# Reordering the opening of a one-core cross-attention and FFN kernel: other matmuls between a tile and its reader, waits at the readers, Wo group 0 beside Wq

## The chip, the cores and the metric

The kernel runs on one core of a Trainium2 chip, and its time is the device time of one execution in microseconds. Three executions of the kernel before took 855.80, 855.86 and 856.62 us (median 855.86).

## What is computed

Eight batches of 128 tokens of width 512 are normalised, attend with 32 query heads (4 key/value heads, head size 128) over a context of 128 rows per batch and over themselves, and go through a gated FFN with fake-quantised weights and activations. Cut to what matters:

```
hidden = concat([context, latents], axis=1)            # latents = layernorm(x)
q = (latents @ Wq)   # 512 x 4096: 4 groups of 8 heads
k, v = hidden @ Wk, hidden @ Wv                         # 512 x 512 each
attn = softmax(einsum('bqhgd,bkhd->bhgqk', q, k) / sqrt(128))
x = x + (attn @ v).reshape(b, q_len, 4096) @ Wo
x = x + ffn(layernorm(x))   # gate, up, down with block-quantised weights, act_qdq between
```

## The kernel before, in words

Every f32 operand is split into an upper f16 part, written by ScalarE (`hi`, L552), and a lower f16 part, written by VectorE (`lo`, L742), and every product is three f16 matmuls (`three`, L313). All reads of a PSUM bank by these two together are called its eviction here; the buffer is free once VectorE's half is through.

All order is written out by hand, engine by engine; waits are counts on semaphores. Each engine's program of the opening walks the same 32 slots, one per key or value tile:

- slots 0 to 7: keys of the context (the first four interleaved by contraction chunk, L351 to L359), slots 8 to 15: its values, with the transposes of the normalised x between them from slot 12 on (`transpose_x`);
- slots 16 to 23: keys of x (`k_tile`), in banks 0 to 3. ScalarE and VectorE evict the tile and split one piece of Wq group 0 (`wq_upper`, `wq_lower`) in each slot;
- then query tiles 0 to 3 (`q_first`, `q_second`, two heads each, banks 6 and 7), scores 0 and 1 (`scores`, banks 0 to 3), on the other engines all ahead of slot 24;
- slots 24 to 31: values of x, eight tiles of 12 matmuls in banks 4 and 5 (the loop `for i in range(B)` of the tensor program). One piece of Wo group 0 is split in each slot (`wo_upper`, `wo_lower`). Reciprocals, products with them (`normalise`, GpSimd) and the splits of P for steps 0 and 1, and the stages of weight unit 3, lie between (`units_in`; a unit is a 128 x 512 piece of an FFN weight that is quantised here and stored to DRAM);
- query tiles 4 and 5, and the loop over 64 steps.

A loop step t holds scores t+2, the Wo product of step t-1 (`project`), query tile t+6 and the product with the values (`head_out`), whose operand comes through a DMA transpose of P (`turn_p`, issued by SP). SP also issues every load, in program order. Wq and Wo pieces have two landing buffers each, so a load n of either waits until piece n-2 is split. `keep_warm` multiplies zeros into a bank that nobody reads.

Its counters in the waits that the change touches: `kv_free` rises by one with each evicted key or value tile and starts at 4 (28: all keys of x are out, 35 and 36: value tiles 6 and 7 too); `q_lo` rises with each evicted query tile; scores 0 want 2, scores 1 want 4; query tile f wants f-1, its bank's last user.

Of the kernel before, what the change touches and what calls it, by code (L numbers as in the profile page):

```python
# [19 lines left out]
B, T, H = 8, 128, 512  # L20
# [61 lines left out]
def build(nc, x, ctx_t, wq, wk, wv, wo, w_units, w_ready, out):  # L82
    stack = ExitStack()
    with stack:
# [94 lines left out]
        kv_mm, kv_hi, kv_free = sem("kv_mm"), sem("kv_hi"), sem("kv_free")  # L179
# [44 lines left out]
        def _(sp):  # L224
# [12 lines left out]
            def load_wo(n):  # L237
                if n >= 2:
                    sp.wait_ge(wo_lo, n - 1)
                sp.dma_start(wo_raw[:, n % 2], wo[n * D:(n + 1) * D, :]).then_inc(wo_loaded[n % 2], 16)  # L240
# [23 lines left out]
            for slot in range(32):  # L264
                if 17 < slot <= 23:
                    load_wq(slot - 16)
                if 25 < slot <= 31:
                    load_wo(slot - 24)
                for v in units_in(slot, 4):
                    store_unit(v)  # L270
                for v in units_in(slot, 1):
                    load_unit(v + 1)
# [39 lines left out]
        def _(pe):  # L312
# [29 lines left out]
            def keep_warm(n):  # L342

                for _ in range(n):
                    nc.tensor.matmul(banks[OB][:, :], warm[:, 0:P], warm[:, :], start=True, stop=True)  # L345

            pe.wait_ge(warm_set, 1)
            keep_warm(8)

            pe.wait_ge(kv_free, NG)  # L350
            for c in range(HC):  # L351
# [31 lines left out]
            def q_first(f):  # L383

                if f % QUADS < 4:
                    pe.wait_ge(wq_lo, f // QUADS * GH + 2 * (f % QUADS) + 2)
                if f >= 2:
                    pe.wait_ge(q_lo, f - 1)
                q_head(f, 0)

            def q_second(f):

                q_head(f, 1).then_inc(q_mm, 1)
# [18 lines left out]
            def head_out(t):  # L412

                g, b = t // QUADS, t % QUADS // 2
                pe.wait_ge(pt_loaded[t % 2], 16 * (t // 2 + 1))
                for c in range(2):
                    for n, (i, r) in enumerate(((0, 0), (0, 1), (1, 0))):
                        mm = nc.tensor.matmul(banks[OB][:, :], kv[:, g + 1, 2 + i, (c * B + b) * P:(c * B + b + 1) * P],  # L418
                                              pt_s[:, t % 2, r, c, :], start=c == 0 and n == 0, stop=c == 1 and n == 2)
                mm.then_inc(pv_mm, 1)  # L420

            def project(t):

                par, hq = t // QUADS % 2, t % 2
                if t % QUADS == 0:
                    pe.wait_ge(wo_lo, t // QUADS * GH + GH)
                if hq == 0 and t >= 2:
                    pe.wait_ge(y_add, t // 2)
                pe.wait_ge(o_hi, t + 1)
                for hh in range(4):  # L430
                    for r in range(2):
                        nc.tensor.matmul(banks[YB][:, :], o_s[:, 0, hh * P:(hh + 1) * P], wo_s[:, par, r, hq * 4 + hh, :],  # L432
                                         start=hq == 0 and hh == 0 and r == 0, stop=False)
                pe.wait_ge(o_lo, t + 1)
                for hh in range(4):
                    mm = nc.tensor.matmul(banks[YB][:, :], o_s[:, 1, hh * P:(hh + 1) * P], wo_s[:, par, 0, hq * 4 + hh, :],  # L436
                                          start=False, stop=hq == 1 and hh == 3)
                mm.then_inc(wo_mm, 1)
# [6 lines left out]
                    mm = nc.tensor.transpose(banks[QB + b % 2][:, c * P:(c + 1) * P], xln2[:, b, c * P:(c + 1) * P], ident[:, :])  # L445
                mm.then_inc(x2_mm, 1)

            pe.wait_ge(xt_free, 12)
            pe.wait_ge(kv_free, 28)
            for f in range(4):  # L450
                q_first(f)
                q_second(f)
                if f == 1:
                    scores(0)
                if f == 3:
                    scores(1)
            for i in range(B):
                if i >= 2:
                    pe.wait_ge(kv_free, 27 + i)
                three(banks[OB + i % 2][:, :], lambda r, c: src_t[:, 5, r, c, i * P:(i + 1) * P],  # L460
                      lambda r, c: wkv_s[:, 1, r, c, :], HC).then_inc(kv_mm, 1)
            for f in range(4, Q_AHEAD):
                q_first(f)
                q_second(f)
            pe.wait_ge(kv_free, 36)
            for t in range(STEPS):
                f = t + Q_AHEAD
                if t + AHEAD < STEPS:
# [81 lines left out]
        def _(act):  # L550
# [67 lines left out]
            for slot in range(32):  # L618
                if slot == 24:
                    q_upper(0)  # L620
                    q_upper(1)
                    exps(0)
                    q_upper(2)
                    q_upper(3)
                    exps(1)
                if slot < 8:
                    k_hi(slot + 1, 0, slot // 4, slot % 4, slot)
                elif slot < 16:
                    v_hi(slot + 1, (slot - 8) * P, slot % 4)
                    if slot >= 12:  # L630
                        xt_upper(2 * (slot - 12))
                        xt_upper(2 * (slot - 12) + 1)
                elif slot < 24:
                    if slot == 16:
                        act.wait_ge(wv_lo, 1)
                    k_hi(slot + 1, 1, (slot - 16) // 4, slot % 4, slot % 4)
                    wq_upper(slot - 16)
                else:
                    v_hi(slot + 1, TOK + (slot - 24) * P, OB + slot % 2)
                    wo_upper(slot - 24)  # L640
                for v in units_in(slot, 2):
                    unit_hi(v)
                if slot == 25:
                    p_upper(0)
# [94 lines left out]
        def _(dve):  # L739
# [136 lines left out]
            for slot in range(32):  # L876
# [10 lines left out]
                if slot == 24:  # L887
                    q_lower(0)
                    q_lower(1)
                    maxima(0)  # L890
                    q_lower(2)
                    reciprocals(0)
                    q_lower(3)
                    maxima(1)
                if slot < 8:
                    k_lo(slot + 1, 0, slot // 4, slot % 4, slot)
                    if slot == 0:
                        dve.wait_ge(x_loaded, 16)
                    nc.vector.bn_stats(bn[:, slot, :], y[:, slot, :]).then_inc(ln_stat, 1)
                elif slot < 16:  # L900
                    v_lo(slot + 1, (slot - 8) * P, slot % 4)
                    if slot >= 12:
                        xt_lower(2 * (slot - 12))
                        xt_lower(2 * (slot - 12) + 1)
                elif slot < 24:
                    k_lo(slot + 1, 1, (slot - 16) // 4, slot % 4, slot % 4)
                    wq_lower(slot - 16)
                else:
                    v_lo(slot + 1, TOK + (slot - 24) * P, OB + slot % 2)
                    wo_lower(slot - 24)  # L910
                if slot == 25:
                    reciprocals(1)
                if slot == 26:
# [331 lines left out]
```

## Time and profile before

| | us |
|---|---|
| median of three executions | 855.86 |
| the profiled execution: span | 855.7 |
| lowest and highest of the three | 855.80, 856.62 |
| opening up to the loop's first matmul | 119.96 |
| attention loop to the last step's products | about 120 to 619 |
| FFN | about 628 to the end |
| PE busy | 786.4 |
| VectorE, ScalarE, GpSimd busy | 630.4, 456.0, 248.8 |

The profiled execution has no time of its own beside its span, which lies 0.16 us under the median. The page gives busy time by engine and by fortieths of the span. A timeline gives instructions in order of time, neighbours of one line merged, with the idle time of their engine ahead of them in brackets. A view by stage gives busy time in chosen stretches, with the granted TensorE clock.

### The profile page before, as it was taken

What the parts mean: (1) busy time and instruction counts of PE and PEld (TensorE: products, weight loads), DVE (VectorE), ACT (ScalarE), POOL (GpSimd) and SP (SyncE); (2) the same over time, 40 slices, a digit from 0 to 9 for tenths busy, and PEclk for the clock granted to TensorE, in tenths of its full rate; (3) what the DMA queues carried; (4) which work ended last, traced back from release to release, by engine and by line L of the source; (5) the groups of instructions that cost most, each with busy time, mean ns of one, the idle gap of its engine ahead of it and who ended that gap; (6) DMA issues with size and microseconds to landing.
All of it is one profiled execution on the core that took longest, in us unless ns stands there. A gap on an engine that the chain in (4) does not pass through costs nothing. (4 is left out here: it accounts for less than half of the span.)

```text
span 855.7 us, 12659 instructions
## 1 busy us (share of the span) xinstructions
PE 786.4 (92%) x4747; PEld 467.2 (55%) x4747; DVE 630.4 (74%) x1148; ACT 456.0 (53%) x968; POOL 248.8 (29%) x380
## 2 busy tenths in 40 slices
PE   8998999999999999999999999998799999701998
PEld 3455466666666666666666666664344444300443
DVE  5874467888777778767878778997485589999741
ACT  5253456655656555656655555554340079695730
POOL 0210313356334455443366334343100012112000
PEclk9999999999999999999999999999899999955999
DMA  9121155757446665465575458787270000000010
GB/s 317 64 75 50 42 131 119 170 133 160 99 111 148 160 139 142 91 150 134 140 169 124 95 128 162 143 171 142 51 135 0 1 1 1 0 1 0 25 38 37
DMA packets 203437, 85.50 MB, mean 100 GB/s; under 512 B 170352, under 2 KB 186736, under 8 KB 203376
## 3 DMA queue, kind: packets, MB, share of 16 engines
q1 hardware_dynamic: 203376, 84.69, 43.3%
q8 instruction: 37, 0.61, 0.3%
q14 instruction: 24, 0.20, 0.1%
HBM read 31.72 MB, written 10.75 MB: 50 GB/s over the span
## 5 line engine op out<-in xcount | busy, mean ns | idle before, releaser
L318 PE MATMUL bank<-arena 128*128 128x256 f16 (+1 forms) x1872 | 261.0, 292 | 3.7 <-DVE arena L742 2.1
L318 PEld LDWEIGHTS bank<-arena 128*128 128x128 f16 x1872 | 182.8, 98 | 85.5 <-DVE arena L742 3.7
L1127 POOL TENSOR_SCALAR arena<-arena,rsum 128x256 f32<-128x256 f32 x256 | 132.7, 518 | 312.0 <-DVE rsum L808 297.9
L742 DVE SCALAR_TENSOR_TENSOR arena<-bank,arena 128x512 f16<-128x512 f32 x168 | 114.7, 689 | 117.7 <-ACT arena L552 117.3
L552 ACT ACTIVATE arena<-bank 128x512 f16<-128x512 f32 x168 | 98.8, 598 | 172.6 <-PE bank L418 95.6
L742 DVE SCALAR_TENSOR_TENSOR arena<-arena 128x512 f16<-128x512 f32 (+4 forms) x196 | 171.4, 886 | 15.8 <-ACT arena L552 15.6
L552 ACT ACTIVATE arena<-arena 128x512 f16<-128x512 f32 (+5 forms) x172 | 135.5, 809 | 61.2 <-POOL arena L1127 19.1
L594 ACT ACTIVATE arena<-bank,nmax 128x256 f32<-128x256 f32 x256 | 117.6, 471 | 60.3 <-DVE nmax L800 60.1
L432 PE MATMUL bank<-arena 128*128 128x512 f16 x512 | 122.7, 383 | 1.5 <-ACT arena L552 1.5
L494 PE MATMUL bank<-arena 128*128 128x512 f16 x528 | 114.1, 379 | 0.0
L408 PE MATMUL bank<-arena 128*128 128x256 f16 x768 | 94.3, 273 | 2.8 <-DVE arena L742 2.8
L418 PE MATMUL bank<-arena 128*128 128x512 f16 x384 | 93.4, 379 | 2.8 <-DMA arena<-arena 2.8
L494 PEld LDWEIGHTS bank<-arena 128*128 128x128 f16 x528 | 51.7, 98 | 62.3 <-issue 0.2
L408 PEld LDWEIGHTS bank<-arena 128*128 128x128 f16 x768 | 75.0, 98 | 12.7 <-DVE arena L742 3.4
L797 DVE TENSOR_REDUCE nraw<-bank 128x4 f32<-128x1024 f32 x64 | 78.3, 1224 | 3.2 <-PE bank L408 3.2
L432 PEld LDWEIGHTS bank<-arena 128*128 128x128 f16 x512 | 50.2, 99 | 50.4 <-issue 2.5
L436 PE MATMUL bank<-arena 128*128 128x512 f16 x256 | 66.2, 381 | 0.0
L669 ACT ACTIVATE arena<-arena,qc 128x1024 int32<-128x1024 f32 (+5 forms) x58 | 55.5, 986 | 16.4 <-DVE qc L990 16.4
L345 PE MATMUL bank<-warm 128*128 128x512 f16 x48 | 17.2, 534 | 47.9 <-DVE worst L968 46.5
L418 PEld LDWEIGHTS bank<-arena 128*128 128x128 f16 x384 | 37.2, 98 | 36.7 <-DMA arena<-arena 4.7
L544 PE MATMUL bank<-arena 128*128 128x512 f16 x264 | 57.1, 379 | 0.0
L594 ACT ACTIVATION_READ_ACCUMULATOR arena<-bank,nmax 128x1 f32 x256 | 51.8, 203 | 0.0
(99 smaller groups left out, 579.6 us busy)
## 6 DMA issues: line engine op xcount, KB each, us to landing
arena<-in_w_units SPq DMA_DIRECT2D x33, 256.0 KB, 3.6
w_ready<-arena SPq DMA_DIRECT2D x33, 256.0 KB, 3.2
arena<-in_wq SPq DMA_DIRECT2D x32, 256.0 KB, 3.5
arena<-in_wo SPq DMA_DIRECT2D x32, 256.0 KB, 3.6
arena<-in_x SPq DMA_DIRECT2D x1, 2048.0 KB, 15.0
out<-arena SPq DMA_DIRECT2D x8, 256.0 KB, 2.0
arena<-in_wk SPq DMA_DIRECT2D x4, 256.0 KB, 4.8
arena<-in_ctx_t SPq DMA_DIRECT2D x4, 256.0 KB, 5.4
```

The source lines that it names most:

```text
L318: last = nc.tensor.matmul(bank, a(i, c), b(j, c), start=start and c == 0 and n == 0, stop=stop and c == chunks - 1 and n == 2)
L408: mm = nc.tensor.matmul(o, q_s[:, buf, i, h, (b % 2) * P:(b % 2) * P + P], kv5[:, g + 1, r, :, b * P:(b + 1) * P], start=n == 0, stop=n == 2)
L418: mm = nc.tensor.matmul(banks[OB][:, :], kv[:, g + 1, 2 + i, (c * B + b) * P:(c * B + b + 1) * P], pt_s[:, t % 2, r, c, :], start=c == 0 a ...
L432: nc.tensor.matmul(banks[YB][:, :], o_s[:, 0, hh * P:(hh + 1) * P], wo_s[:, par, r, hq * 4 + hh, :], start=hq == 0 and hh == 0 and r == 0, ...
L436: mm = nc.tensor.matmul(banks[YB][:, :], o_s[:, 1, hh * P:(hh + 1) * P], wo_s[:, par, 0, hq * 4 + hh, :], start=False, stop=hq == 1 and hh ...
L494: mm = nc.tensor.matmul(banks[t % 4][:, :], wgu[:, m * FT + t, i, c * P:(c + 1) * P], xq[:, j, c, th * 512:(th + 1) * 512], start=c == 0 a ...
L544: mm = nc.tensor.matmul(banks[b % 4][:, :], oq[:, h, t, b * P:(b + 1) * P], wd_s[:, t, r, :], start=t == 0 and m == 0, stop=t == FT - 1 an ...
L552: return nc.scalar.activation(dst, src, ACT.Copy, scale=scale)
L594: nc.scalar.activation(p_s[:, t % 2, :, hh, :], bank[:, (hh % 2) * 256:(hh % 2) * 256 + 256].rearrange("p (c t) -> p c t", c=2), ACT.Exp, ...
L742: return nc.vector.scalar_tensor_tensor(out=dst, in0=src, scalar=scale, in1=part, op0=ALU.mult, op1=ALU.subtract)
L797: nc.vector.tensor_reduce(nraw[:, :], psum[:, s:s + 2, :].rearrange("p b (h t) -> p (b h) t", h=2), AX.X, ALU.max, negate=True).then_inc(n ...
L1127: done = nc.gpsimd.tensor_scalar(p_s[:, t % 2, :, hh, :], p_s[:, t % 2, :, hh, :], rsum[:, t % 2, hh:hh + 1], P_SCALE, ALU.mult, ALU.mult)
```

## The change

- TensorE: query tiles 0 to 2, then the wait for all keys of x, scores 0, query tile 3, value tile 0 of x, scores 1, value tiles 1 to 7. The wait for all value evictions ahead of the loop becomes two, in `head_out` and `project` of step 0.
- ScalarE and VectorE follow that order: exponentials and maxima of step 0 behind the eviction of query tile 2, those of step 1 behind the eviction of value tile 0.
- Wo group 0 is loaded and split in slots 16 to 23 beside Wq.
- Ten matmuls on zeros at the start instead of eight.

```
@@ sync
             for slot in range(32):
                 if 17 < slot <= 23:
                     load_wq(slot - 16)
-                if 25 < slot <= 31:
-                    load_wo(slot - 24)
+                    load_wo(slot - 16)
@@ tensor
-            keep_warm(8)
+            keep_warm(10)
@@ head_out
+                if t == 0:
+                    pe.wait_ge(kv_free, 35)
@@ project
+                if t == 0:
+                    pe.wait_ge(kv_free, 36)
@@ tensor
-            pe.wait_ge(xt_free, 12)
-            pe.wait_ge(kv_free, 28)
-            for f in range(4):
-                q_first(f)
-                q_second(f)
-                if f == 1:
-                    scores(0)
-                if f == 3:
-                    scores(1)
-            for i in range(B):
+            def x_value_tile(i):
+
                 if i >= 2:
                     pe.wait_ge(kv_free, 27 + i)
                 three(banks[OB + i % 2][:, :], lambda r, c: src_t[:, 5, r, c, i * P:(i + 1) * P],
                       lambda r, c: wkv_s[:, 1, r, c, :], HC).then_inc(kv_mm, 1)
+
+            pe.wait_ge(xt_free, 12)
+            for f in range(3):
+                q_first(f)
+                q_second(f)
+            pe.wait_ge(kv_free, 28)
+            scores(0)
+            q_first(3)
+            q_second(3)
+            x_value_tile(0)
+            scores(1)
+            for i in range(1, B):
+                x_value_tile(i)
             for f in range(4, Q_AHEAD):
                 q_first(f)
                 q_second(f)
-            pe.wait_ge(kv_free, 36)
@@ scalar, slot 24
                     q_upper(0)
                     q_upper(1)
+                    q_upper(2)
                     exps(0)
-                    q_upper(2)
                     q_upper(3)
-                    exps(1)
@@ scalar, slots 16 to 23, then 24 to 31
                     wq_upper(slot - 16)
+                    wo_upper(slot - 16)
                 else:
                     v_hi(slot + 1, TOK + (slot - 24) * P, OB + slot % 2)
-                    wo_upper(slot - 24)
+                    if slot == 24:
+                        exps(1)
@@ vector, slot 24
                     q_lower(0)
                     q_lower(1)
+                    q_lower(2)
                     maxima(0)
-                    q_lower(2)
                     reciprocals(0)
                     q_lower(3)
-                    maxima(1)
@@ vector, slots 16 to 23, then 24 to 31
                     wq_lower(slot - 16)
+                    wo_lower(slot - 16)
                 else:
                     v_lo(slot + 1, TOK + (slot - 24) * P, OB + slot % 2)
-                    wo_lower(slot - 24)
+                    if slot == 24:
+                        maxima(1)
```

TensorE from the last keys of x to the loop, before. The 128x256 rows of L318 are query tiles (24 matmuls each), its 128x512 rows are key and value tiles (12 each), L408 is a score step:

```order
L318 MATMUL bank<-arena 128x512 x96
L318 MATMUL bank<-arena 128x256 x48
L408 MATMUL bank<-arena 128x256 x12
L318 MATMUL bank<-arena 128x256 x48
L408 MATMUL bank<-arena 128x256 x12
L318 MATMUL bank<-arena 128x512 x96
L318 MATMUL bank<-arena 128x256 x48
L408 MATMUL bank<-arena 128x256 x12
```

The same stretch in the changed kernel, where these lines are L317 and L407:

```order
L317 MATMUL bank<-arena 128x512 x96
L317 MATMUL bank<-arena 128x256 x72
L407 MATMUL bank<-arena 128x256 x12
L317 MATMUL bank<-arena 128x256 x24
L317 MATMUL bank<-arena 128x512 x12
L407 MATMUL bank<-arena 128x256 x12
L317 MATMUL bank<-arena 128x512 x84
L317 MATMUL bank<-arena 128x256 x48
L407 MATMUL bank<-arena 128x256 x12
```

A third query tile now stands ahead of scores 0, and a value tile between query tile 3 and scores 1. No matmul is added or lost here.

SP from the first in-slot load of Wq (L235) to the first transpose of P (L254), before; L245 and L249 are the load and the store of a weight unit:

```order
L235 DMA arena<-in_wq 128x4x128 x6
L240 DMA arena<-in_wo 128x512
L245 DMA arena<-in_w_units 128x512
L240 DMA arena<-in_wo 128x512 x3
L249 DMA w_ready<-arena 128x1024
L240 DMA arena<-in_wo 128x512 x2
L254 DMA_TRANSPOSE arena<-arena 128x16x128
```

And changed:

```order
L235 DMA arena<-in_wq 128x4x128
L240 DMA arena<-in_wo 128x512
L235 DMA arena<-in_wq 128x4x128
L240 DMA arena<-in_wo 128x512
L235 DMA arena<-in_wq 128x4x128
L240 DMA arena<-in_wo 128x512
L235 DMA arena<-in_wq 128x4x128
L240 DMA arena<-in_wo 128x512
L235 DMA arena<-in_wq 128x4x128
L240 DMA arena<-in_wo 128x512
L235 DMA arena<-in_wq 128x4x128
L240 DMA arena<-in_wo 128x512
```

Here the loads of Wo alternate with those of Wq; behind them come a unit's load, its store and the first transpose, with nothing between.

ScalarE from query tile 0 on, before (L552 is `hi`, of a bank 128x512 a query tile, of a bank 128x4x128 a value tile, of the arena 128x512 a Wo piece, 128x1024 P; L594 the exponentials):

```order
L552 ACTIVATE arena<-bank 128x512 x2
L594 ACTIVATE arena,psums<-bank,nmax 128x2x128 x4
L552 ACTIVATE arena<-bank 128x512 x2
L594 ACTIVATE arena,psums<-bank,nmax 128x2x128 x4
L552 ACTIVATE arena<-bank 128x4x128
L552 ACTIVATE arena<-arena 128x512
L552 ACTIVATE arena<-bank 128x4x128
L552 ACTIVATE arena<-arena 128x512
L552 ACTIVATE arena<-arena 128x1024
```

And changed, where the lines are L559 and L601:

```order
L559 ACTIVATE arena<-bank 128x512 x3
L601 ACTIVATE arena,psums<-bank,nmax 128x2x128 x4
L559 ACTIVATE arena<-bank 128x512
L559 ACTIVATE arena<-bank 128x4x128
L601 ACTIVATE arena,psums<-bank,nmax 128x2x128 x4
L559 ACTIVATE arena<-bank 128x4x128
L559 ACTIVATE arena<-arena 128x1024
L559 ACTIVATE arena<-bank 128x4x128 x2
```

No Wo piece stands between the value tiles any more, the exponentials of step 0 stand ahead of the eviction of query tile 3, and those of step 1 ahead of the eviction of value tile 1.

## Rows read from the trace of the kernel before

**Rows 1.** The page: busy us, share of the span, instructions of TensorE.
```profile
PE 786.4 (92%) x4747; PEld 467.2 (55%) x4747; DVE 630.4 (74%) x1148; ACT 456.0 (53%) x968; POOL 248.8 (29%) x380
```
**Rows 2.** By stage: window, length, busy us of each engine, granted clock, DMA share, GB/s.
```profile
9.90:18.00 8.10, 8.10 (x39) 3.70 (x38) 4.42 (x5) 5.20 (x6) 0.50 (x1) 1.00 1.05 392
120.00:520.00 400.00, 400.00 (x2770) 270.76 (x2768) 311.16 (x540) 237.97 (x612) 179.89 (x280) 1.00 0.59 133
603.00:607.00 4.00, 4.00 (x10) 1.36 (x9) 1.23 (x1) 1.90 (x3) 0.00 (x0) 0.50 0.21 42
```
**Rows 3.** Timeline of TensorE: start, us, what, count, [idle before it <- releaser].
```profile
52.92 20.88 PE L318 MATMUL bank<-arena 128*128 128x512 f16 x96
75.26 5.40 PE L318 MATMUL bank<-arena 128*128 128x256 f16 x48 [1.46 <-issue]
82.08 1.48 PE L408 MATMUL bank<-arena 128*128 128x256 f16 x12 [1.42 <-DVE arena L742]
...
90.21 1.48 PE L408 MATMUL bank<-arena 128*128 128x256 f16 x12 [1.42 <-DVE arena L742]
91.53 13.11 PE L318 MATMUL bank<-arena 128*128 128x512 f16 x60
105.24 2.76 PE L318 MATMUL bank<-arena 128*128 128x512 f16 x12 [0.59 <-DVE arena L742]
109.53 10.59 PE L318 MATMUL bank<-arena 128*128 128x512 f16 x72 [1.53 <-DVE arena L742]
119.96 1.47 PE L408 MATMUL bank<-arena 128*128 128x256 f16 x12
```
**Rows 4.** Timeline of ScalarE, then of VectorE, between 74 and 108 us.
```profile
85.06 0.47 ACT L594 ACTIVATE arena<-bank,nmax 128x256 f32<-128x256 f32 x1 [3.77 <-DVE nmax L800]
...
86.87 0.61 ACT L552 ACTIVATE arena<-bank 128x512 f16<-128x512 f32 x1
...
107.12 1.15 ACT L552 ACTIVATE arena<-arena 128x512 f16<-128x512 f32 x2 [4.43 <-DMA arena<-in_wo]
...
74.47 0.69 DVE L742 SCALAR_TENSOR_TENSOR arena<-bank,arena 128x512 f16<-128x512 f32 x1 [1.30 <-ACT arena L552]
...
100.74 2.02 DVE L742 SCALAR_TENSOR_TENSOR arena<-arena 128x512 f16<-128x512 f32 x2
```
**Rows 5.** GpSimd: timeline at 99 us, then all 33 of L1151 (ns min/median/max).
```profile
99.01 2.67 POOL L1127 TENSOR_SCALAR arena<-arena,rsum 128x256 f32<-128x256 f32 x4 [8.49 <-DVE rsum L808]
101.76 1.90 POOL L1151 TENSOR_TENSOR arena<-arena,winv 128x512 f32<-128x512 f32 x1
...
L1151 POOL TENSOR_TENSOR arena<-arena,winv x33: 1046/1048/1897, 28.9 to 565.4; 128x512 f32<-128x512 f32 x33
```
**Rows 6.** SP's issues of Wo at 104 us; landings of L240, 90 to 600, then all.
```profile
104.07 4.76 SPq L240 DMA_DIRECT2D arena<-in_wo  x3
...
DMA to landing us min/median/max: 2.5/3.6/5.1
...
DMA to landing us min/median/max: 2.5/3.6/10.6
```
**Rows 7.** Timeline of the first 40 us: TensorE, its weight loads, VectorE.
```profile
1.44 3.59 PE L345 MATMUL bank<-warm 128*128 128x512 f16 x8 [1.44 <-POOL warm L1118]
5.77 12.47 PE L356 MATMUL bank<-arena 128*128 128x512 f16 x48 [0.73 <-DVE arena L742]
...
9.88 7.87 PEld L356 LDWEIGHTS bank<-arena 128*128 128x128 f16 x37 [0.16 <-issue]
...
39.05 2.27 PEld L318 LDWEIGHTS bank<-arena 128*128 128x128 f16 x12 [0.59 <-DVE arena L742]
...
14.82 2.29 DVE L742 SCALAR_TENSOR_TENSOR arena<-arena 128x2048 f16<-128x2048 f32 x1 [3.26 <-ACT arena L552]
...
21.05 0.70 DVE L899 BATCH_NORM_STATS2 bn<-arena 128x6 f32<-128x512 f32 x1 [0.62 <-DMA arena<-in_x]
```
**Rows 8.** Timeline of TensorE ahead of the second norm's transposes.
```profile
601.03 1.94 PE L445 MATMUL bank<-ident,arena 128*128 128x128 f32 x8 [2.96 <-ACT arena L605]
```

## The prediction, made before the changed kernel had run

> **What bounds the kernel now.** I read the page first, then the busy time by stage, then TensorE's timeline of the opening. The page has PE busy 92% of the span [rows 1]. By stage, PE is busy 400.00 of 400.00 us from 120 to 520 [rows 2]. So the attention loop is a wall of matmuls: it costs what it costs from the moment it starts, and what is taken out ahead of it arrives at the end unless something behind it takes it back. The opening is where PE still waits. Its timeline [rows 3] shows five rows with idle time ahead of them between the end of the last K tile and the loop, whose first instruction is the row at 119.96:
>
> - 1.46 us before the first query tile: the four query tiles stand behind one wait for the last K eviction;
> - 1.42 us before scores 0 and 1.42 before scores 1: each reads the query tile multiplied just before it, which ScalarE and VectorE have yet to evict;
> - 0.59 and 1.53 us inside the value tiles.
>
> The modelled end of a row lies 0.16 us past the start of a row that follows without a wait (109.53 + 10.59 = 120.12, next start 119.96), so each bracket understates its loss by 0.16. The five cost 6.42 + 5 x 0.16 = 7.22 us. The work itself, from the same rows: a value tile (12 matmuls) 12 x (13.11 - 0.16)/60 = 2.59 us, a query tile 24 x (5.40 - 0.16)/48 = 2.62, a score step 1.48 - 0.16 = 1.32.
>
> **The change, part by part.**
>
> 1. *The query tiles no longer wait for the last K eviction.* They write banks 6 and 7, the K tiles 0 to 3. K tiles end at 52.92 + 20.88 - 0.16 = 73.64 and query tile 0 starts there. The wait now stands before scores 0, at about 81.5; the eviction is through at 75.2, when the query tiles start today. Gain 1.62.
>
> 2. *Query tile 2 between tile 1 and scores 0.* Tile 1 ends at 78.88, tile 2 at 81.50. From the end of a query tile to its reader is 82.08 - 80.50 = 1.58 us (the two halves of an eviction and what signals between them), so tile 1 is ready at 80.46, 1.0 early. Tile 2 itself needs tile 0 out of bank 6: 76.26 + 1.58 = 77.84, again 1.0 early. Gain 1.58.
>
> 3. *Value tile 0 between query tile 3 and scores 1.* Scores 0 end at 82.82, tile 3 at 85.44, value tile 0 at 88.03. ScalarE does the exponentials of step 0 ahead of evicting tile 3. Today they start 1.66 after the scores end (83.40 to 85.06) and the eviction follows 1.81 later [rows 4]: 84.48, then 86.29, and the two halves of an eviction, 0.60 and 0.69, end near 87.65. Scores 1 may start at 87.7 and are wanted at 88.03. This is the thinnest cover of the opening, 0.3 us; without it the cost is what the exponentials are late. Gain 1.58.
>
> 4. *Wo group 0 beside Wq.* Today ScalarE stands 4.43 us before 107.12 for a Wo piece whose load SP could issue only at 104.07, behind the load of a weight unit that waits for GpSimd's product, done at 103.66 [rows 4, 5, 6]; every value eviction queues behind that, and PE's 1.53 is its last link. The change takes all eight Wo pairs and six SP issues out of the value stage. They move under the K tiles, where each slot of 2.59 us carries a K eviction and a Wq piece: with a Wo piece beside them ACT goes from 2 x 0.60 to 1.8 us a slot and VectorE from 2 x 0.69 to 2.1, both below 2.59. SP issues twelve loads there for six, some 0.4 us each. In the last slot VectorE's K half ends at 75.16 [rows 4], Wq's at 75.8 and Wo's at 76.4; query tile 0 ends at 76.26 and its eviction finds both engines free. Gain of the 1.53: 1.69 with the overlap.
>
> 5. *What is late next.* The 0.59 is another chain: reciprocals 1, four products on GpSimd, the unit's product, VectorE's two rounding steps, and only then the eviction that value tile 5 needs. Redone with today's times: scores 1 end at 89.35, exponentials run from 91.0 to 92.8, value tile 1 is evicted and the reciprocals are out by 94.1, GpSimd's four products run from 94.3 to 97.0 (2.67 [rows 5]). The unit's product follows. It took 1.90 us here against a median of 1.05 [rows 5], and VectorE was in the lower halves of P and of a Wo piece, 2.02 us from 100.74 [rows 4], for its first 1.0. P's half alone is some 1.3: after value tile 2 (94.53, evicted 1.4 later) it runs from 95.95 to 97.25. If the unit's product must only outlast that, it ends at 98.3 and value tile 5 starts 1.58 later (103.66 to 105.24 today), at 99.9, wanted at 99.71: 0.2 lost. If 1.90 is its price, it ends at 98.9 and 0.8 is lost. I take 0.2, since 1.05 is the median of 33 and the Wo half is gone. The Trainium skill (SBUF — State Buffer, on the shared port pair) says that a GpSimd instruction and a VectorE one with two SBUF inputs exclude each other for a whole instruction. By that rule the first reading holds (with the second the sum would be 0.6 less, 849.4). The trace agrees: 1.0 of overlap, 0.85 lost. Gain 0.75 - 0.2 = 0.55.
>
> 6. *The waits at their readers.* The final wait for all value evictions held nothing (no bracket at 119.96), so placing it at head_out and project gains and costs nothing. Behind it stand scores 2 and a query head, which do not need it.
>
> 7. *Ten warming matmuls instead of eight.* Eight take 3.59 - 0.16 from 1.44, 0.43 us each, to 4.87, and the first real matmul is at 5.77 [rows 7]. Two more end at 5.72: cost 0 to 0.1. They fill the idle 0.9 us. The real matmuls issue every 0.43 (512 columns: 1.2 GHz) until 9.88, where weight loads begin to follow without a gap, and every 0.216 (2.4 GHz) after it. I price an earlier rise at nothing, because value tile 4 of the context waits for VectorE just before 39.05 [rows 7], and VectorE's chain there hangs on the landing of x at 21.05, not on PE. PE earlier only waits longer there. The Trainium skill (TensorE: Matmul & The Clock Gate, Part 1) says that the slow state is the default and sustained activity releases it; by it the ten would bring the rise forward. The first matmuls at half clock cost at most ten times 0.21 us, and the half K tiles cannot start before VectorE has split their operand, 14.82 + 2.29 = 17.1, 1.0 before today's 5.77 + 12.47 - 0.16 = 18.1. By the rule, were it passed on, the sum would be 1.0 better.
>
> **The sum.** 1.62 + 1.58 + 1.58 + 1.69 + 0.55 = 7.02; the loop starts near 112.9 instead of 119.96. The profiled span is 855.7 us and the median of the runs 855.86, a difference of 0.16 that I carry along: 855.86 - 7.02 = **848.8 us**.
>
> **The rivals.**
>
> *A, part of the gain is eaten in the opening.* Against it, the covers of 1.0 and 0.3 us worked out above. For it, two new round trips. Wo pieces use two buffers, so piece 7 is split after three rounds of landing plus 1.4 us, from an issue at about 60.9: 65.1 + 3L, and query tile 2 may start 0.7 after that. It wants 78.88, so it is held from L = 4.36. Landings in the loop are 2.5 to 5.1, median 3.6 [rows 6]. At 5.1 every time PE loses 3 x 0.74 = 2.2; with the 0.6 that point 5 leaves open, 851.6.
>
> *B, slower.* The same mechanism past its point: if six more loads in this stage made all landings exceed 6.7 us, query tile 2 would be held by more than the 7.02 gained, and the kernel is slower; at 7.5, towards the longest Wo landing of the run (10.6, in the opening's flood of loads [rows 6]), it is 855.86 - 7.02 + 9.4 = 858.2. Against it: the engines moved 392 GB/s in that flood [rows 2], and 512 KB per 2.59 us, what is asked here, is half of it.
>
> *C, the late clock drop goes.* From 603 to 607 the granted clock is 0.50 (1.2 GHz) and ten matmuls take the 4.00 us [rows 2, 8], after PE had idled 2.96. At the upper level each is 0.21 shorter: about 2.1 us, on the path to the second norm. The kernel gets there 7 us earlier; if the drop comes at another moment it may vanish: 846.7. Nothing in the change attacks it.
>
> *D, the early clock rise is passed on:* 847.8, the skill's rule of point 7 beside it. It needs VectorE not to be the wall at 39.
>
> *E, the moved text does nothing:* the order of instructions on PE, ACT and SP is different in the build, so only point 6 is void.
>
> **How the numbers follow.** Forecast 0.66, A 0.16, B 0.03, C 0.09, D 0.05, E 0.01. The range runs from C (846.7) to A's price (851.6); outside lie B, E and some of the tails, about 0.1. A measurement of this kernel can tell 0.2%, 1.7 us, from nothing. Faster by more: 0.95; within: 0.02; slower: 0.03.
>
> **What would show it.** Right: the loop's first matmul near 112.9, no brackets above 0.3 us on PE between 73.6 and there but a small one at the sixth value tile, GpSimd's unit product near 1.1, ACT never waiting for in_wo, PE full from 113 on. Wrong: a bracket before the third query tile (Wo late), before scores 1 (exponentials late), or PE idle in the loop, which would mean that it was not the wall there. If the loop starts on time and the end is off by 2 us, look at the granted clock at 595 to 620.

## The result, and the profile after

The changed kernel took 849.04 us (median of 4, 848.73 to 849.15) against 855.97 of the kernel before beside it: ratio 0.9922, 95% interval 0.991 to 0.9934. That is 0.8% faster, and clear of noise. Run again it took 849.21 (848.97 to 850.23, 6 runs) against 855.78: 0.9926, 0.9915 to 0.9938. The forecast was 848.8, in 846.7 to 851.6.

The opening of the changed kernel on TensorE's timeline, the rows that answer to [rows 3] and to the first two of [rows 7]:

```profile
1.45 3.80 PE L344 MATMUL bank<-warm 128*128 128x512 f16 x10 [1.45 <-POOL warm L1127]
6.01 10.52 PE L355 MATMUL bank<-arena 128*128 128x512 f16 x48 [0.76 <-DVE arena L750]
17.00 20.89 PE L317 MATMUL bank<-arena 128*128 128x512 f16 x96 [0.47 <-DVE arena L750]
38.88 2.76 PE L317 MATMUL bank<-arena 128*128 128x512 f16 x12 [0.99 <-DVE arena L750]
...
52.74 28.74 PE L317 MATMUL bank<-arena 128*128 128x512 f16 x168
81.32 1.47 PE L407 MATMUL bank<-arena 128*128 128x256 f16 x12
82.63 5.37 PE L317 MATMUL bank<-arena 128*128 128x256 f16 x36
87.84 1.47 PE L407 MATMUL bank<-arena 128*128 128x256 f16 x12
89.15 10.52 PE L317 MATMUL bank<-arena 128*128 128x512 f16 x48
100.03 13.19 PE L317 MATMUL bank<-arena 128*128 128x512 f16 x84 [0.36 <-DVE arena L750]
113.05 1.47 PE L407 MATMUL bank<-arena 128*128 128x256 f16 x12
```

From 38.88 to the loop one bracket is left, 0.36 us before value tile 5. The last K tiles and query tiles 0 to 2 are one row (x168: 96 and 72 matmuls), and so no wait lies between them. The loop starts at 113.05 instead of 119.96, 6.91 us earlier; 7.02 were forecast. The loop is still a wall, in the view by stage:

```profile
112.90:520.00 407.10, 407.10 (x2820) 275.77 (x2819) 317.38 (x551) 241.96 (x623) 183.19 (x285) 1.00 0.60 133
```

The two profiled spans, 855.7 and 847.4, are 8.3 us apart, not 6.9, and the other 1.4 must not be read as gain. The recorded time of each execution here is 1.7 to 1.9 us above its span (849.15 for 847.4; 853.93 and 855.51 for spans of 852.1 and 853.7 of the kernel before). By that the profiled execution of the kernel before took some 857.5, an estimate, while its times ran from 853.8 to 857.0 beside the runs here. Of the 1.4, 1.1 lies between the loop's start and the FFN: at [rows 8] and in the window of 603 to 607 in [rows 2] that execution had ten slow matmuls at a granted clock of 0.50, and the first FFN matmul came 508.45 us after the loop's first (628.41). In the changed kernel it came 507.31 after (620.36). The last 0.3 lies in the FFN and was not looked into. The row that answers to [rows 8], and what follows it:

```profile
594.27 1.41 PE L448 MATMUL bank<-ident,arena 128*128 128x128 f32 x8 [3.00 <-ACT arena L612]
595.47 3.33 PE L435 MATMUL bank<-arena 128*128 128x512 f16 x8
598.64 1.03 PE L439 MATMUL bank<-arena 128*128 128x512 f16 x4
```

The eight are still slow (3.33 us, against 1.89 at the upper clock), the four behind them no longer.

### The profile page after: what moved, and what is told of

It reads as the page before. It is cut to its first block and busy times, and to the rows that moved or that the text cites. A ratio compares the mean times of both kernels' runs of the same rounds, so it can differ in the third digit from the quotient of the medians.

```text
span 847.4 us, 12664 instructions
## 1 busy us (share of the span) xinstructions
PE 781.1 (92%) x4749; PEld 465.7 (55%) x4749; DVE 630.1 (74%) x1148; ACT 456.3 (54%) x968; POOL 249.0 (29%) x380
## 5 line engine op out<-in xcount | busy, mean ns | idle before, releaser
L317 PE MATMUL bank<-arena 128*128 128x256 f16 (+1 forms) x1872 | 260.6, 292 | 1.8 <-DVE arena L750 1.8
L317 PEld LDWEIGHTS bank<-arena 128*128 128x128 f16 x1872 | 182.9, 98 | 83.3 <-DVE arena L750 3.3
L559 ACT ACTIVATE arena<-bank 128x512 f16<-128x512 f32 x168 | 98.7, 598 | 165.6 <-PE bank L419 94.3
L559 ACT ACTIVATE arena<-arena 128x512 f16<-128x512 f32 (+5 forms) x172 | 135.4, 810 | 62.6 <-POOL arena L1136 19.2
L601 ACT ACTIVATE arena<-bank,nmax 128x256 f32<-128x256 f32 x256 | 117.6, 471 | 57.2 <-DVE nmax L808 57.2
L407 PE MATMUL bank<-arena 128*128 128x256 f16 x768 | 94.3, 273 | 0.0
L407 PEld LDWEIGHTS bank<-arena 128*128 128x128 f16 x768 | 75.1, 98 | 9.6
L344 PE MATMUL bank<-warm 128*128 128x512 f16 x50 | 15.5, 475 | 48.0 <-DVE worst L977 46.5
L601 ACT ACTIVATION_READ_ACCUMULATOR arena<-bank,nmax 128x1 f32 x256 | 51.8, 202 | 0.0
```

The lines of the kernel that those rows point to most:

```text
L317: last = nc.tensor.matmul(bank, a(i, c), b(j, c), start=start and c == 0 and n == 0, stop=stop and c == chunks - 1 and n == 2)
L407: mm = nc.tensor.matmul(o, q_s[:, buf, i, h, (b % 2) * P:(b % 2) * P + P], kv5[:, g + 1, r, :, b * P:(b + 1) * P], start=n == 0, stop=n == 2)
L559: return nc.scalar.activation(dst, src, ACT.Copy, scale=scale)
L601: nc.scalar.activation(p_s[:, t % 2, :, hh, :], bank[:, (hh % 2) * 256:(hh % 2) * 256 + 256].rearrange("p (c t) -> p c t", c=2), ACT.Exp, ...
```

## The experiments

The start of the loop is read from each run's profile. The stretch that ends there and starts with the keys of x (52.74 in the change) scatters still less: it took 60.31 or 60.32 us in all five profiles whose edits touch nothing in it, and 67.04 in the kernel before. The keys of x themselves started anywhere from 52.51 to 52.84 with ten warming matmuls and the weight units in their old slots. The times of one kernel scatter over 0.4 to 4.8 us.

The runs fall in groups, each on a chip of its own with the kernel before beside it. The medians of the kernel before were 855.51 beside Wo back, only Wo moved, eight warming matmuls and scores 1 direct; 854.4 beside K wait ahead, GpSimd's products later, units later and the zeros in step 62; 855.58 beside scores 1 direct on all engines, more loads and the last three together; 855.78 beside the change again. The second group's base is thus 1.1 to 1.6 lower than that of the change, and a plain difference of medians between the two mixes this in; the ratios do not.

| run | loop starts | keys of x to loop | median us | lowest to highest | ratio to before, interval |
|---|---|---|---|---|---|
| the change | 113.05 | 60.31 | 849.04 | 848.73 to 849.15 | 0.9922 (0.991 to 0.9934) |
| the change again | 112.86 | 60.31 | 849.21 | 848.97 to 850.23 | 0.9926 (0.9915 to 0.9938) |
| Wo back in the value slots | 114.96 | 62.45 | 850.39 | 849.93 to 851.0 | 0.9941 (0.993 to 0.9953) |
| only Wo moved | 117.36 | 64.58 | 853.0 | 851.4 to 853.98 | 0.9968 (0.9957 to 0.998) |
| eight warming matmuls | 113.49 | 60.31 | 849.08 | 847.53 to 849.58 | 0.9922 (0.991 to 0.9934) |
| scores 1 direct | 116.14 | 63.60 | 852.49 | 852.2 to 854.48 | 0.9975 (0.9964 to 0.9986) |
| scores 1 direct, all engines | 114.87 | 62.03 | 850.07 | 848.88 to 853.71 | 0.9948 (0.993 to 0.9966) |
| K wait ahead | 114.68 | 61.93 | 850.1 | 848.59 to 851.04 | 0.9939 (0.9923 to 0.9956) |
| GpSimd's products later | 112.53 | 59.78 | 847.7 | 847.0 to 848.29 | 0.9915 (0.9902 to 0.9928) |
| units later | 112.06 | 60.32 | 847.29 | 846.06 to 848.54 | 0.991 (0.9892 to 0.9927) |
| matmuls on zeros in step 62 | 112.98 | 60.32 | 847.7 | 847.1 to 847.9 | 0.9913 (0.9899 to 0.9927) |
| more loads | 115.98 | 63.45 | 852.42 | 849.6 to 853.01 | 0.9964 (0.995 to 0.9978) |
| the last three gains together | 111.44 | 59.78 | 846.26 | 845.31 to 847.94 | 0.9901 (0.9886 to 0.9915) |

**Wo back in the value slots.**

```
-                    load_wo(slot - 16)
+                if 25 < slot <= 31:
+                    load_wo(slot - 24)
... wo_upper and wo_lower from slots 16 to 23 back to 24 to 31
```

> The changed kernel with Wo group 0 back in the value slots 24 to 31 (loads, ScalarE's and VectorE's pieces); the matmul order stays new. Theory (SP cannot issue Wo piece 3 before GpSimd's unit product is done, ScalarE waits for it and the eviction of value tile 4 behind it): a wait of ScalarE for in_wo of 2 us or more comes back near 100 us, value tile 6 starts 1.5 us late or more, the loop starts at 114.5 to 115.4 instead of 113.05, time 850.5 to 851.4 against 849.0. Rival (the new matmul order alone carries the gain): loop at 113.1, 849.0.

ScalarE's timeline of that run has the wait back, and TensorE's has two large brackets in the value tiles:

```profile
102.12 1.15 ACT L560 ACTIVATE arena<-arena 128x512 f16<-128x512 f32 x2 [4.30 <-DMA arena<-in_wo]
```
```profile
101.26 2.76 PE L318 MATMUL bank<-arena 128*128 128x512 f16 x12 [1.49 <-DVE arena L751]
104.53 10.59 PE L318 MATMUL bank<-arena 128*128 128x512 f16 x72 [0.51 <-DVE arena L751]
114.96 1.47 PE L408 MATMUL bank<-arena 128*128 128x256 f16 x12
```

SP issued the late piece at 99.13, behind the unit's load at 98.75. ScalarE's wait for it ended at 102.12, the eviction of value tile 4 came behind it, and value tile 6, which needs that, started at 104.53. In the change it starts 2.59 behind value tile 5, at 102.62. These 1.9 us are the whole loss.

The bracket of 1.49 stands earlier, before value tile 5, and cannot come from that wait, which had not ended by then. It is VectorE's own queue, which has the lower halves of Wo pieces back:

```profile
97.06 2.74 DVE L751 SCALAR_TENSOR_TENSOR arena<-arena 128x512 f16<-128x512 f32 x2 [0.40 <-ACT arena L560]
...
100.52 0.68 DVE L751 SCALAR_TENSOR_TENSOR arena<-bank,arena 128x512 f16<-128x512 f32 x1
```

The row of 2.74 is the lower half of a Wo piece and that of P; behind it come the two rounding steps and, at 100.52, the eviction that value tile 5 needs. The load is later still and hides this one; with the load in time and the halves left there, value tile 5 would still have been late. The loop is 1.9 later (2.1 from the keys of x), and the median, 850.39, lies just below the 850.5 expected. By the ratios, 0.9941 and 0.9922, the Wo move is worth 1.6 us in the new order.

**Only Wo moved**, in the kernel before.

> The kernel before with nothing but Wo group 0 moved beside Wq. Theory: the idle 1.46, 1.42 and 1.42 us of TensorE stay, the 0.59 and the 1.53 inside the value tiles go; loop at 117.5 to 118.3 instead of 119.96, time 853.5 to 854.3 against 855.97. Rival (the Wo loads beside Wq make ScalarE late for the query tiles): a longer idle time before the second score step's chain, loop later than 118.5.

The loop starts 2.60 earlier than in the kernel before (2.46 from the keys of x) and the median is 853.0, both a little better than expected. The three brackets of 1.46, 1.42 and 1.42 stay, and the eight value tiles and two query tiles are one row:

```profile
75.13 5.40 PE L317 MATMUL bank<-arena 128*128 128x256 f16 x48 [1.46 <-issue]
81.94 1.48 PE L407 MATMUL bank<-arena 128*128 128x256 f16 x12 [1.42 <-DVE arena L741]
...
90.08 1.48 PE L407 MATMUL bank<-arena 128*128 128x256 f16 x12 [1.42 <-DVE arena L741]
91.40 26.12 PE L317 MATMUL bank<-arena 128*128 128x512 f16 x144
```

Both the 0.59 and the 1.53 are gone, although the order of matmuls is the old one.

**K wait ahead.**

```
             pe.wait_ge(xt_free, 12)
+            pe.wait_ge(kv_free, 28)
             for f in range(3):
                 q_first(f)
                 q_second(f)
-            pe.wait_ge(kv_free, 28)
```

> The changed kernel with the wait for the last K eviction back ahead of the query tiles. Theory: query tile 0 starts at 75.1 to 75.3 instead of 73.5, everything behind it 1.6 to 1.8 later, loop at 114.7, time 850.7. Rival (the later covers had slack that swallows it): less than 1 us slower.

The bracket of 1.46 is back before the query tiles and the loop is 1.63 later. The median of 850.1 is 1.1 above that of the change, less than the 1.7 expected, but its base was lower too: the ratios, 0.9939 and 0.9922, are 1.5 us apart. Their intervals overlap, so the place and its size on TensorE are shown, and the time agrees with them.

**Scores 1 direct.** First on TensorE alone, then with ScalarE and VectorE in the same order:

```
-            x_value_tile(0)
             scores(1)
+            x_value_tile(0)
... second run also: exps(1) and maxima(1) ahead of slot 24's eviction
```

> The changed kernel with scores 1 directly behind query tile 3, value tile 0 behind them. Theory: scores 1 wait for the eviction of query tile 3, 2.2 us behind scores' place (ScalarE does the exponentials first), and the chain reciprocals, GpSimd, rounding then has one value tile more ahead of value tile 5, so its 0.36 us of idle time goes: net loop at 114.3 to 115.0, time 850.2 to 851.0. Rival (the cover is not needed): unchanged 849.0.

> As the run with scores 1 directly behind query tile 3, but with the maxima and exponentials of step 1 ahead of the eviction of value tile 0 on ScalarE and VectorE, in the order of TensorE. Theory (the idle time of 2.24 us at scores 1 is the missing cover; the rest of what that run lost was the other engines waiting for value tile 0 first): idle 2.08 at scores 1 stays, no other idle time in the value tiles, loop at 114.3 to 115.0 instead of 116.14, time 850.2 to 851.2. Rival (the idle times in the value tiles have another cause): loop above 115.5.

The first run missed its expectation: the loop at 116.14 is 1.1 later than the latest expected, and the median 1.5 above. I had left ScalarE's order alone: it evicts value tile 0 ahead of the exponentials of step 1, and so waited for a tile that TensorE now multiplies later. With all engines in one order the loop starts at 114.87, and TensorE's timeline has one bracket:

```profile
82.72 2.78 PE L317 MATMUL bank<-arena 128*128 128x256 f16 x24
87.59 1.48 PE L407 MATMUL bank<-arena 128*128 128x256 f16 x12 [2.08 <-DVE arena L749]
88.91 26.12 PE L317 MATMUL bank<-arena 128*128 128x512 f16 x144
```

The value tile covers 2.24 us (2.08 and the 0.16) and not 1.58. Only one query tile stands behind scores 0 now, where the kernel before had two; it ended at 85.34 while ScalarE was in the exponentials of step 0 until 86.20. The loop is 1.82 later than in the change and not 2.24, since with a later scores 1 the bracket before value tile 5 goes, as expected. A mirrored order on the engines that evict is worth another 1.3 (1.6 from the keys of x).

**Eight warming matmuls.**

```
-            keep_warm(10)
+            keep_warm(8)
```

> The changed kernel with eight warming matmuls instead of ten. Theory (VectorE's chain after the landing of x is the wall at value tile 4 of the context, whatever TensorE did before): value tile 4 starts within 0.2 us of 38.9 and the time stays within 0.3 us of 849.0. Rival (an earlier rise of the clock is passed on): 0.5 to 1.0 us slower, 849.5 to 850.0, with value tile 4 later.

The median did not move (849.08). The clock did. With eight, the weight loads of the three profiled executions (the kernel before, only Wo moved, this one) are a slow 0.43 us apart until 9.88, 9.55 and 10.82, and the second four K tiles of the context start at 18.0 to 18.6. With ten they become fast between 4.0 and 7.4 in the profiled executions of all eleven kernels and repeats that have ten, and these K tiles start at 16.8 to 17.2. Weight loads of the run with eight, then of the change:

```profile
10.82 3.13 PEld L355 LDWEIGHTS bank<-arena 128*128 128x128 f16 x15 [0.28 <-issue]
```
```profile
4.41 0.34 PEld L344 LDWEIGHTS bank<-warm 128*128 128x128 f16 x2 [0.28 <-issue]
```

Value tile 4 of the context started at 38.88 in the change and, by its row at 18.61 and 96 x 0.2157, at 39.3 with eight. So 1.6 us at the second four K tiles became 0.4 there: VectorE is the wall for the other 1.2. The 0.4 is more than the 0.2 expected, and the loop starts 0.44 later. In the run with eight no bracket stands before value tile 4, so there TensorE itself came last.

**Units later**, which takes that wall down.

```
-SLOT_OF = (5, 9, 13, 25)
+SLOT_OF = (8, 11, 14, 25)
```

> The changed kernel with weight units 0 to 2 started in slots 8, 11 and 14 instead of 5, 9 and 13, so that none stands in VectorE's chain ahead of the layer norm. Theory (that chain is what value tile 4 of the context waits for, 0.99 us of idle time at 38.88): the idle time goes or falls below 0.2, the loop starts at 112.0, time 847.9 to 848.4. Rival (the landing of x alone sets it, or the units' stages now stall the transposes): no gain, or idle time at the transposes and 849 or more.

The bracket at value tile 4 is gone, and the loop starts at 112.06:

```profile
17.16 23.48 PE L317 MATMUL bank<-arena 128*128 128x512 f16 x108
40.48 1.04 PE L338 MATMUL bank<-ident,arena 128*128 128x128 f32 x8
```

The median, 847.29, is lower than expected; its four runs fall in two pairs, 846.1 and 846.3, 848.3 and 848.5. By the ratios, 0.991 and 0.9922, the gain is 1.0 us, which is that of the loop's start, with overlapping intervals.

**GpSimd's products later.**

```
-                if slot == 26:
-                    normalise(1)
... and behind unit_dequantise:
+                if slot == 27:
+                    normalise(1)
```

> The changed kernel with GpSimd's four products of step 1 behind the stages of weight unit 3 instead of ahead of them. Theory (the idle time before value tile 5 is the end of the chain reciprocals, four products 3.19 us, unit product, rounding): no idle time of TensorE before value tile 5, loop at 112.5, time 848.5. Rival (the wait is for something else): 0.36 stays, 849.0.

No bracket before value tile 5, the loop at 112.53, 0.52 earlier, which is the bracket of 0.36 and the 0.16. The place is shown. The median is 1.3 lower, but beside a lower base: the ratios, 0.9915 and 0.9922, are 0.6 us apart, which is about the 0.52, and their intervals overlap.

**Matmuls on zeros in step 62.**

```
                 for b in X2_AT.get(t, ()):
... ahead of it:
+                if t == 62:
+                    pe.wait_ge(exp_out, 4 * 62 + 4)
+                    for _ in range(10):
+                        nc.tensor.matmul(banks[SC][:, :], warm[:, 0:P], warm[:, :], start=True, stop=True)
```

> The changed kernel with ten matmuls on zeros ahead of the transposes of loop step 62, where TensorE idles 3.00 us. Theory (that idle time lets the granted clock fall, and the slow matmuls behind it are on the path to the second norm): granted clock 1.00 from 585 to 610, the eight matmuls of the projection there 1.9 us instead of 3.3, the stretch to the first FFN matmul 1.3 to 1.6 us shorter in the profiled execution, time 847.5 to 848.4. Rival (the matmuls on zeros run longer than the idle time, or the slow stretch is hidden): 849.0 or up to 0.5 more.

By stage, the change and then this run:

```profile
594.00:598.00 4.00, 3.73 (x14) 2.01 (x15) 1.49 (x2) 2.99 (x6) 1.86 (x4) 0.62 0.69 130
```
```profile
594.00:598.00 4.00, 3.70 (x21) 2.19 (x22) 1.45 (x2) 2.98 (x6) 1.90 (x4) 1.00 0.69 130
```

21 matmuls instead of 14 in 4 us, the granted clock at 1.00, the first FFN matmul 506.02 after the loop's start instead of 507.31: the slow stretch is on the path. This distance is 505.95 and 506.02 in the two profiles with these zeros and 506.70 to 508.45 in the twelve without. The median is 1.3 lower, but by the ratios, 0.9913 and 0.9922, only 0.8, with overlapping intervals, so the gain is shown in the profiles and not in the times.

The idle time of 3.00 us is not the whole cause, though. In the run with the units later the same 3.00 stands before the same transposes, and the twelve matmuls behind them are fast (1.89 and 1.03 us); the slow ones come one step later, behind 2.17 us of idle time:

```profile
593.11 1.12 PE L448 MATMUL bank<-ident,arena 128*128 128x128 f32 x8 [3.00 <-ACT arena L612]
594.07 1.89 PE L435 MATMUL bank<-arena 128*128 128x512 f16 x8
...
600.29 0.66 PE L448 MATMUL bank<-ident,arena 128*128 128x128 f32 x4 [2.17 <-DVE arena L859]
600.78 3.00 PE L435 MATMUL bank<-arena 128*128 128x512 f16 x8
```

With the zeros in step 62 neither place is slow. What decides at which of the two the clock falls was not settled.

**More loads**, to move the landings and nothing else that is read:

```
                     load_wo(slot - 16)
+                    for i in range(2):
+                        k = 2 * (slot - 18) + i
+                        if k >= 4:
+                            sp.wait_ge(dummy[k % 4], 16 * (k // 4))
+                        sp.dma_start(f32(160 + 2 * (k % 4), 512), wo[i * D:(i + 1) * D, :]).then_inc(dummy[k % 4], 16)
... and ScalarE waits for all of them ahead of exps(0)
```

> The changed kernel with two more loads of 256 KB, which nobody reads, behind each Wo load of slots 18 to 23 (twelve in all), so that the pieces of Wq and Wo land later. Theory (piece 7 is split after three rounds of landing plus 1.4 us from 60.9, and query tile 2 needs ScalarE and VectorE behind it): landings of 5 to 7 us, TensorE idles before query tile 2 or before scores 0 by 3 x (L - 4.36), that is 2 to 8 us, loop at 115 to 121, time 851 to 857. Rival (there is slack that the sum did not see, or the landings do not grow): no idle time there, 849.

The view of DMA issues from 58 to 80, in the change and in this run, and TensorE's row at query tile 2:

```profile
arena<-in_wq SPq DMA_DIRECT2D x6, 256.0 KB, 3.7
arena<-in_wo SPq DMA_DIRECT2D x6, 256.0 KB, 3.8
```
```profile
arena<-in_wo SPq DMA_DIRECT2D x18, 256.0 KB, 5.5
arena<-in_wq SPq DMA_DIRECT2D x6, 256.0 KB, 5.2
```
```profile
81.64 2.78 PE L323 MATMUL bank<-arena 128*128 128x256 f16 x24 [2.98 <-DVE arena L758]
```

At a landing of 5.2 to 5.5 the sum gives 3 x (5.35 - 4.36) = 3.0; measured are 2.98 + 0.16. So rival A's mechanism is real. By the sum the change keeps 0.6 us of landing from its point. By its trace it is less: VectorE was through with query tile 0 at 77.60, and query tile 2 started near 78.7, so 1.1 us were in hand, about 0.4 for each of the three rounds.

**The last three gains together.**

> The changed kernel with all three of: GpSimd's products of step 1 behind unit 3, weight units 0 to 2 in slots 8, 11 and 14, and ten matmuls on zeros ahead of the transposes of step 62. Theory (three separate places): the gains add, loop at 111.4 to 111.6, the stretch from the loop to the first FFN matmul 506.0 us, time 845.2 to 846.2 against 849.04. Rival (what is saved in the opening is lost behind it): 847 or more.

Loop at 111.44, first FFN matmul 505.95 after it, median 846.26, just above the range expected for it, and the fastest of all: 2.8 below the change and 2.95 below its repeat. The marks give 1.61 and 1.36, 2.97 together. By the ratios, 0.9901 against 0.9922 and 0.9926, it is 1.8 to 2.1, and the intervals just overlap; no execution of the combined version was as slow as the fastest of the change (847.94, 848.73).

> The changed kernel unchanged, as a base for the others, since the kernel before has had medians from 854.4 to 856.0 beside them. Theory: its executions spread over some 2 us like those of the kernel before, the loop starts at 113.0 to 113.5 in the profiled one, median 848.2 to 849.2. Rival (the combined version gained nothing over it): median of 847 or less.

The repeat lies at the upper end of what was expected (849.21; its loop, at 112.86, starts a little earlier than expected), so the combined version's gain is not a high day of the change.

## Why the prediction was right

The mechanism held part by part, and the time came out 0.2 us from the forecast. Some of that closeness is luck. In the stretch from the keys of x to the loop the gain was 6.73 us (67.04 to 60.31) and not 7.02, because point 5 was sized 0.3 too small; another 0.18 came in ahead of that stretch, where the sum had nothing, and that much is also within what this place scatters between executions. The sentence that span and median lie 0.16 apart compared two unlike things: times are 1.8 above spans, and the profiled execution was, by the estimate above, some 1.6 above the median. The forecast started from the median; from that execution's own time it would have been 850.5.

1. *K wait:* 1.62 forecast, 1.63 by its undoing.
2. *Query tile 2 ahead of scores 0:* no bracket at 81.32 where 1.42 stood. It was not undone alone; the timeline shows it.
3. *Value tile 0:* forecast to gain 1.58 with 0.3 us in hand. VectorE was through at 87.43 and scores 1 started at 87.84, so 0.4 in hand. Taken away alone it leaves 2.24 of idle time, because point 2 moved a query tile ahead of scores 0 and only one is left to run beside the exponentials; the loop is 1.82 later.
4. *Wo:* the wait for the load is as told, from SP to TensorE's 1.53. What the forecast gave to point 5 alone is partly Wo too: only Wo moved took away the 0.59 as well as the 1.53, and with Wo back VectorE's queue alone held value tile 5 by 1.49. ScalarE's waits in the change from 52 to 113 have no in_wo. They have, which I had not said, five waits for in_wq (us in all, times, longest):

```profile
ACT arena L559 <- DMA arena<-in_wq: 4.3, 5, 1.5
```

Two loads a slot land in 3.7 and 3.8 us instead of the 2.8 of Wq alone before. That used up part of the cover, and none was passed on.

5. *The chain before value tile 5* was sized 0.3 too small (0.52 lost, 0.2 forecast). The unit's product took 1.05 as told. The term that failed is the four products ahead of it, which took 3.19 us and not 2.67:

```profile
94.13 3.19 POOL L1136 TENSOR_SCALAR arena<-arena,rsum 128x256 f32<-128x256 f32 x4 [5.46 <-DVE rsum L816]
97.41 1.05 POOL L1160 TENSOR_TENSOR arena<-arena,winv 128x512 f32<-128x512 f32 x1
```
```profile
95.77 1.22 DVE L750 SCALAR_TENSOR_TENSOR arena<-arena 128x1024 f16<-128x1024 f32 x1
```

VectorE's lower half of P, 1.22 us with both inputs in SBUF, ran inside them. The four of step 0 took 2.13 (86.54) beside an eviction, which reads a PSUM bank and one tile of SBUF, so 1.06 of the 1.22 was added. The rule of the Trainium skill (SBUF — State Buffer, on the shared port pair) fits with the trace here too: it was I who held it against one GpSimd instruction only and kept the old 2.67 for the others. The price can fall on VectorE as well: with Wo back the four products took 2.13, and the lower half of P took 2.07 us beside GpSimd's unit product.

6. *The waits at their readers:* nothing forecast, and no bracket stands at 113.05 or in the wall behind it. They were not undone alone.

7. *Ten warming matmuls:* the rise came at 4.0 to 7.4 instead of 9.5 to 10.8, and most of it ended at VectorE, as forecast: by the run with eight 1.2 of 1.6, the other 0.4 reached the loop, and in the median nothing is to be seen. Rival D was wrong here. With the units later the wall is gone and the loop starts a further 1.0 earlier; that the early rise would then count in full is argued from its row without a bracket, since eight warming matmuls were not run with it. TensorE: Matmul & The Clock Gate of the Trainium skill, Part 1, has sustained activity release the throttle, and the trace agrees.

The sum was 7.02 and the loop started 6.91 earlier. Rival B did not come, since landings of 3.8 are far from 6.7. Rival C came in part: the slow stretch varies from execution to execution, and it can be removed, but the change did not remove it.

## What to carry to other kernels

Where a tile is read right after it is written, put independent matmuls between, and give the engines that evict it the same order: the mismatch cost 1.3 us on top of the missing cover. When a split of a loaded tile moves away, count what it took from the engine's queue and not only the wait for its load. Before adding loads to a stage, turn the buffers' round trips into a landing time at which the first consumer is held; here it was 4.4 us by the sum, some 0.2 less by the trace, and the run with more loads met the sum. When runs are taken in groups, compare their ratios to a common kernel beside them. Take a forecast from the median and use a profiled span for differences inside it only.

## What had not been expected

- Two more matmuls on zeros at the start moved the rise of the clock from 9.5 to 10.8 us down to 4.0 to 7.4, with idle time of 0.76 us still in the change's profile. Why two matmuls do that in every profiled execution was not settled.
- GpSimd's four products took 2.13, 2.67 and 3.19 us in three places; the 3.19 is put down to the instruction that VectorE ran beside them, the 2.67 was not looked into further.
- Executions of the kernel before differ by up to 3 us (853.8 to 857.0), those of one run by 4.8. A part of it is probably how slow the stretch behind the loop is: between the loop's start and the FFN, profiled executions without the zeros in step 62 differ by up to 1.8 us (506.70 to 508.45).
